# The first cross-attention of a two-layer decoder: head placement by DMA copies in place of zero-padded projections

## What is computed

```python
def _L0_xattn_ref(query, key_value, Wq, bq, Wk, bk, Wv, bv, Wo, bo):
    H = 16
    D = Cq // H                      # 256 // 16 = 16
    scale = D ** (-0.5)
    q = (query @ Wq + bq).reshape(B, Nq, H, D).transpose(0, 2, 1, 3)
    k = (key_value @ Wk + bk).reshape(B, Nkv, H, D).transpose(0, 2, 1, 3)
    v = (key_value @ Wv + bv).reshape(B, Nkv, H, D).transpose(0, 2, 1, 3)
    attn = jnp.clip(jnp.einsum('bhqd,bhkd->bhqk', q, k) * scale, -1e4, 1e4)
    attn = jax.nn.softmax(attn, axis=-1)
    x = jnp.einsum('bhqk,bhkd->bqhd', attn, v).reshape(B, Nq, Cq)
    return x @ Wo + bo

x = _layernorm(x + _L0_attn_ref(x, ...))
x = _layernorm(x + _L0_xattn_ref(x, ctx_768, ...))
```

## Time and profile before

| | us |
|---|---|
| median of three timed runs | 1267.47 (1267.25 to 1268.99) |
| the profiled execution | 1272.5 |
| its span | 1270.6 |
| PE busy | 1150.3 (91%) |
| DVE busy | 719.7 (57%) |
| ACT busy | 565.0 (44%) |
| POOL busy | 105.4 (8%) |

### The profile page before, as it was taken

One profiled execution on the slowest core, in us unless ns is written; L12 is line 12 of the kernel. 1 busy time (PEld: TensorE's weight loads), 2 busy tenths in 40 slices (PEclk: granted clock), 3 DMA queues, 4 the chain that ended last, 5 costly groups with the idle time before them and its releaser, 6 DMA issues.

```text
span 1270.6 us, 19991 instructions
## 1 busy us (share of the span) xinstructions
PE 1150.3 (91%) x7418; PEld 720.2 (57%) x7418; DVE 719.7 (57%) x1054; ACT 565.0 (44%) x1084; POOL 105.4 (8%) x147
## 2 busy tenths in 40 slices
PE   4999999898988988869988999999999999998797
PEld 2453443442222322247866777877787887786465
DVE  4344445667888789661426466465646666673213
ACT  1344344154545555751214566456635564562210
POOL 0112232112100000010001000010001000100100
PEclk7799899898979999979999999999999999999799
DMA  7012212320000000000023233123634964400000
GB/s 205 14 51 100 89 37 100 115 76 1 1 1 1 1 1 1 1 18 1 1 67 112 62 91 74 34 52 83 150 85 100 214 144 101 101 18 1 1 17 17
DMA packets 56962, 74.20 MB, mean 58 GB/s; under 512 B 12443, under 2 KB 33446, under 8 KB 56870
## 3 DMA queue, kind: packets, MB, share of 16 engines
q1 hardware_dynamic: 53110, 69.26, 21.4%
q10 hardware_dynamic: 3760, 3.67, 0.9%
HBM read 36.20 MB, written 15.73 MB: 41 GB/s over the span
## 4 chain that ended last, share of the span: by engine, by line
PE 79%; DVE 9%; issue 5%; ACT 4%; DMA 1%; POOL 1%; SPq 1%; ACTq 0%; POOLq 0%; DVEq 0%
PE p_unit L1665 20%; PE p_ring L1665 12%; PE p_out L1789 9%; PE p_ring L1685 8%; PE p_ring L1766 8%; PE p_ring L1732 7%; PE p_out L1755 6%; DVE halves L1454 2%; PE p_unit L1857 2%; PE p_ring L1710 1%; ACT prob_b L1238 1%; DVE prob_a L1468 1%; DVE x L1560 1%; PE p_ring L1724 1%; PE p_ring L1703 1%
## 5 line engine op out<-in xcount | busy, mean ns | idle before, releaser
L1454 DVE TENSOR_REDUCE halves<-p_ring 128x2 f32<-128x1024 f32 x128 | 156.2, 1220 | 65.8 <-PE p_ring L1710 65.6
L1252 ACT ACTIVATE prob_a<-p_ring 128x1024 f32<-128x1024 f32 x128 | 130.6, 1022 | 101.6 <-PE p_ring L1732 101.4
L1434 DVE TENSOR_REDUCE nmax<-p_ring 128x2 f32<-128x1024 f32 (+1 forms) x128 | 156.0, 1219 | 33.7 <-PE p_ring L1685 33.6
L1270 ACT ACTIVATE probT_b<-p_ring 128x512 f32<-128x512 f32 x144 | 84.5, 598 | 202.2 <-PE p_ring L1766 200.7
L1238 ACT ACTIVATE prob_b<-p_ring,nmax 128x512 f32<-128x512 f32 (+1 forms) x192 | 158.6, 837 | 18.3 <-DVE nmax L1434 18.0
L1685 PE MATMUL p_ring<-stacks 128*128 128x512 f32 x512 | 151.4, 418 | 8.9 <-ACT prob_b L1238 5.3
L1487 DVE COPY probT_b<-p_ring 128x512 f32<-128x512 f32 x112 | 77.1, 688 | 133.5 <-PE p_ring L1766 133.0
L1766 PE MATMUL p_ring<-ident,prob_b 128*128 128x128 f32 x1024 | 134.5, 274 | 0.3 <-ACT probT_b L1270 0.3
L1766 PEld LDWEIGHTS p_ring<-ident,prob_b 128*128 128x128 f32 x1024 | 116.2, 141 | 23.5 <-issue 14.8
L1732 PE MATMUL p_ring<-x_q,x_kq 32*128 32x512 f32 x512 | 124.4, 658 | 2.9 <-DVE halves L1454 2.9
L1454 DVE TENSOR_REDUCE wide_max<-p_ring 128x2 f32<-128x256 f32 (+3 forms) x64 | 52.6, 823 | 90.3 <-PE p_ring L1703 90.3
(11 more groups left out here) (226 smaller groups left out, 1614.1 us busy)
## 6 DMA issues: line engine op xcount, KB each, us to landing
stacks<-x_kd SPq DMA_DIRECT2D x64, 256.0 KB, 5.9
stacks<-splitH_b SPq DMA_DIRECT2D x80, 128.0 KB, 2.3
stacks<-splitL_b SPq DMA_DIRECT2D x80, 128.0 KB, 2.4
x_kd<-early SPq DMA_DIRECT2D x19, 256.0 KB, 2.0
x_v<-x_vd SPq DMA_DIRECT2D x8, 512.0 KB, 4.1
x_kd<-xT SPq DMA_DIRECT2D x13, 256.0 KB, 2.0
x_vd<-early SPq DMA_DIRECT2D x11, 256.0 KB, 2.0
a_st<-a_image SPq DMA_DIRECT2D x64, 32.0 KB, 1.8
```

Source lines behind the costliest of these rows:

```text
L1252: nc.scalar.activation(prob_place(key), slot_of("S2", key), ACT.Exp, accum_out=x0_sums[:, m:m + 1]).then_inc(done["E2"], 1)
L1270: keep_turned(act, key, lambda o, i: nc.scalar.activation(o, i, ACT.Copy)).then_inc(done["VA"], 1)
L1434: nc.vector.tensor_reduce(nmax[:, n % 4, 0:heads], src, AX.X, ALU.max, negate=True).then_inc(done["M"], 1)
L1454: nc.vector.tensor_reduce(to, src, AX.X, ALU.max, negate=True).then_inc(done["M1"], 1)
```

## The change

Queries and keys of X0 are now projected without padding. A batch takes four key units (`kd`: 128 of 256 rows of all heads, by 512 context rows) and two query units (`qd`), 12 in all in place of 24. `kd` goes to the early buffers and, by XO, to a tensor `x0_kd` in DRAM; `qd` goes to `x0_qd` in SBUF. A new step KL on SP, one for each group, then copies each head's 16 rows to its block of 32 in `x0_kq`: four DMAs from `x0_kd` and four from `x0_qd`. It waits for both stores, the queries, and the last S2 of group n − 3. One cast of 128×1536 (KF) follows two ticks later in the schedule. S1 and S2 read 17 rows of a block in place of 32. POOL fills `x0_kq` once at the start with ones and zeros (row 16 stays), DVE's memsets and spreading copies of the weights go, and the two landing tensors for weights go as well. The scale of the queries is applied by ACT as it drains them. The slots of the early buffers are dealt anew; both halves of an X1 key unit are stored after `EL`.

The diff, cut:

```diff
@@ paired_stream
-            if u[0] in ("k", "q") and u[1] == "X0":
-                sched.add("KF", *u)
-            if u[:2] == ("v", "X1"):
+            if u[:2] == ("v", "X1") or u[0] == "kd":
                 sched.add("XO", *u)
@@ build_schedule
+    def x0_keys(b):
+        return [unit("kd", b, m, s) for m in range(2) for s in range(2)]
+
+    def x0_queries(b):
+        return [unit("qd", b, m, after=[turned_x("A0", b)] + ([later(("KL", (0, 2 * m + 1)), 3)] if b else [])) for m in range(2)]
+
+    def x0_operands(b, g):
         n = 4 * b + g - HELD
+        return [step("KL", b, g, after=[UA("qd", b, g // 2), later(("XO", ("kd", b, g // 2, 1)), 1)]
+                     + (used(8 + n) if n >= 0 else [])),
+                step("KF", b, g, after=[later(("KL", (b, g)), 2)])]
...
+        order = [u[1][1:] for u in x0_keys(1)] + order
...
-                slot = sum(early_uses) % EARLY
+                slot = sum(early_uses) % (3 if u[:2] == ("kd", 0) else EARLY)
@@ SP
+                    if u[0] == "kd":
+                        _, b, m, s = u
+                        wait(sp, "UA", *u)
+                        sp.dma_start(x0_kd[b, 128 * m:128 * m + 128, 512 * s:512 * s + 512], early_place(u, 0))\
+                          .then_inc(early_out[early_places[(u, 0)][0]], 16)
...
-                        for part, ready in ((1, "EH"), (0, "EL")):
-                            wait(sp, ready, *u)
+                        wait(sp, "EL", *u)
+                        for part in (1, 0):
...
+                if kind == "KL":
+                    b, g = key
+                    G, place = 8 + 4 * b + g, (4 * b + g) % HELD
+                    sp.wait_ge(x0_cleared, 1)
+                    for s in range(2):
+                        slot, before = early_places[(("kd", b, g // 2, s), 0)]
+                        sp.wait_ge(early_out[slot], 16 * (before + 1))
+                    wait(sp, "UA", "qd", b, g // 2)
+                    if 4 * b + g >= HELD:
+                        wait(sp, "S2", *prob_items(PAIRS[G - HELD])[-1])
+                    for a in range(4):
+                        sp.dma_start(x0_kq[32 * a:32 * a + 16, place, 0:2, :],
+                                     x0_kd[b, 64 * g + 16 * a:64 * g + 16 * a + 16, :].rearrange("r (s n) -> r s n", s=2))\
+                          .then_inc(x0_held[place], 16)
+                        at = 64 * (g % 2) + 16 * a
+                        sp.dma_start(x0_kq[32 * a:32 * a + 16, place, 2, :], x0_qd[at:at + 16, g // 2, :])\
+                          .then_inc(x0_held[place], 16)
@@ POOL
-            pool.wait_ge(x0_scaled, 1)
+            nc.gpsimd.memset(x0_kq[:, :, 0:2, :], 1.0)
+            nc.gpsimd.memset(x0_kq[:, :, 2, :], 0.0).then_inc(x0_cleared, 1)
...
-                    wait(pool, "UA", *u)
-                    if 4 * b + g >= HELD:
-                        wait(pool, "S1", *max_items(PAIRS[8 + 4 * b + g - HELD])[-1])
-                    nc.gpsimd.tensor_copy(x0_kqF[:, place, part, :], x0_kq[:, place, part, :]).then_inc(done["KF"], 1)
+                    pool.wait_ge(x0_held[n % HELD], 16 * 8 * (n // HELD + 1))
+                    if n >= HELD:
+                        wait(pool, "S1", *max_items(PAIRS[8 + n - HELD])[-1])
+                    nc.gpsimd.tensor_copy(x0_kqF[:, n % HELD], x0_kq[:, n % HELD]).then_inc(done["KF"], 1)
@@ ACT
+                    elif u[0] == "qd":
+                        _, b, m = u
+                        act.wait_ge(x0_scaled, 1)
+                        if b:
+                            for g in (2 * m, 2 * m + 1):
+                                act.wait_ge(x0_held[g % HELD], 16 * 8 * (g // HELD + 1))
+                        ins = nc.scalar.activation(x0_qd[:, m, :], p_unit[:, :], ACT.Identity, bias=x0_bq[:, m:m + 1],
+                                                   scale=LAYERS["X0"]["D"] ** -0.5)
@@ DVE
-            nc.vector.memset(x0_wq[:, :, :], 0.0)
-            nc.vector.memset(x0_wk0[:, :], 0.0)
-            link(nc.vector.memset(x0_wk1[:, :], 0.0))
-            nc.vector.memset(x0_wk1[64:65, :].rearrange("p (h r) -> p h r", r=32)[:, :, 16], 1.0)
@@ PE, S1 (S2 alike)
-                            ins = nc.tensor.matmul(o[:, aa, :], x0_kqF[r:r + 32, place, 2, 128 * i:128 * i + 128],
-                                                   x0_kqF[r:r + 32, place, hf, :], start=True, stop=True,
+                            ins = nc.tensor.matmul(o[:, aa, :], x0_kqF[r:r + 17, place, 2, 128 * i:128 * i + 128],
+                                                   x0_kqF[r:r + 17, place, hf, :], start=True, stop=True,
```

More of the change, by code:

```diff
@@ L170, in may_score @@
             return age("DS", L, b, g) >= 3
-        return age("KF", "q", L, b, g) >= 2 and all(age("KF", "k", L, b, g, h) >= 2 for h in range(2))
+        return age("KF", b, g) >= 2
     def ready(item):
@@ L461, in build_schedule @@
         after_attention("A0", 1, "X0"),
[L462 to L465, removed]
+        [unit("cT", sg, c) for sg in range(2) for c in range(2)] + x0_keys(0)
+        + [unit("cT", sg, c) for sg in range(2, 4) for c in range(2)],
+        [q for b in range(B) for q in x0_queries(b)],
+        [s for b in range(B) for g in range(4) for s in x0_operands(b, g)],
         a0_start(1),
@@ L781, in decoder @@
         x1_kv_loaded = sem("x1_kv_loaded")
+        x0_cleared = sem("x0_cleared")
+        x0_held = [sem(f"x0_held{j}") for j in range(HELD)]
         wqk_ready = sem("wqk_ready")
@@ L1135, in _ @@
                 if kind == "KF":
[L1136 to L1142 removed]
+                    b, g = key
+                    n = 4 * b + g
+                    pool.wait_ge(x0_held[n % HELD], 16 * 8 * (n // HELD + 1))
+                    if n >= HELD:
+                        wait(pool, "S1", *max_items(PAIRS[8 + n - HELD])[-1])
+                    nc.gpsimd.tensor_copy(x0_kqF[:, n % HELD], x0_kq[:, n % HELD]).then_inc(done["KF"], 1)
                 elif kind == "EH":
@@ L1317, in _ @@
                         ins = nc.scalar.activation(a0_H[:, u[2], :], p_unit[:, :], ACT.Copy)
-                    elif u[0] in ("q", "k") and u[1] == "X0":
-                        _, L, b, g = u[:4]
-                        place, part = (4 * b + g) % HELD, u[4] if u[0] == "k" else 2
-                        if 4 * b + g >= HELD:
-                            wait(act, "S2", *prob_items(PAIRS[8 + 4 * b + g - HELD])[-1])
-                        if u[0] == "q":
-                            ins = nc.scalar.activation(x0_kq[:, place, part, :], p_unit[:, :], ACT.Identity,
-                                                       bias=x0_bq[:, g:g + 1])
-                        else:
-                            ins = nc.scalar.activation(x0_kq[:, place, part, :], p_unit[:, :], ACT.Copy)
-                    elif u[:2] in (("k", "X1"), ("v", "X1")):
+                    elif u[0] == "qd":
[6 more added lines that the diff above has]
+                                                   scale=LAYERS["X0"]["D"] ** -0.5)
+                    elif u[:2] in (("k", "X1"), ("v", "X1")) or u[0] == "kd":
                         early_free(act, u, 0)
@@ L1704, in _ @@
                     else:
-                        wait(pe, "KF", "q", L, b, g)
-                        wait(pe, "KF", "k", L, b, g, hf)
+                        wait(pe, "KF", b, g)
                         place = (G - 8) % HELD
@@ L1732, in _ @@
                             ins = nc.tensor.matmul(o[:, aa, :],
-                                                   x0_kq[r:r + 32, place, j // 4, 128 * (j % 4):128 * (j % 4) + 128],
-                                                   x0_q2[r:r + 32, G % 2, :], start=True, stop=True,
+                                                   x0_kq[r:r + 17, place, j // 4, 128 * (j % 4):128 * (j % 4) + 128],
+                                                   x0_q2[r:r + 17, G % 2, :], start=True, stop=True,
                                                    tile_position=(r, 0))
```

83 lines of the change are left out of this document (32 added, 51 removed).

## The result

| | median us | range, runs |
|---|---|---|
| before, beside it | 1268.95 | 1267.25 to 1271.73, 6 |
| changed | 1347.41 | 1338.41 to 1349.01, 6 |

The account below looks back on a forecast made before the run. In X0 PE sets the pace with a projection in each tick, DVE without. Terms −23.0 + 3.7 − 2.1 + 3.0 + 3.5 + 1.0 = −13.9 us took 1267.47 to 1253.6 us; range 1244 to 1264.

Parts of the forecast that it names:

- Part 4: X0's scores read 17 rows instead of 32, columns staying 512: nothing, ±1 us in all.
- D: Slower rival: every X0 cast holds a clip all its 1.6 us and brings a half-clock spell; 1272.6 us, chance 0.08.
- Part 1: Five triplets of projections leave X0's loop, 4.42 us each, 5.3 for the first: −23.0 us.
- Part 2: Projections that come back: one query unit at tick 107, two more units in ticks 90–103; +3.7 us.
- Part 3: At the start, memsets leave DVE ahead of a step PE waits for: −2.1 us, bounds 0 and −2.2.
- Part 5: KL's copies, eight DMA issues per group on SP, nothing urgent behind them in X0's loop: costed at nothing.
- Part 6: One fused POOL cast per group in X0: held DVE clips +3.0 us, one new half-clock spell +3.5 us.
- Part 7: Early buffer slots, ticks 93 and 94: ACT's writes of batch 1's x wait for stores; +1.0 us, bounds 0 and 3.
- Rival B: X0's new casts cost nothing, if they fall beside the row reduce: 1247 us, chance 0.20.
- C: Rival: three of five X0 casts bring a half-clock spell, two more than forecast; 1260.6 us, chance 0.17.
- E: Rival: SP queue jams before X0, ticks 64 to 70, so POOL and PE wait for copies; 1260.6 us, chance 0.10.
- wrong altogether: Sign in X0's loop: DMA copies come late, with PE waiting for KF at a group's first S1; no size given.

Follow-up runs that it names:

- 32-row kernel: The changed kernel with X0's scores S1 and S2 reading 32 rows again instead of 17, nothing else: 1246.4 us, ratio 0.982; second series 1241.2 us, 0.977.

## Why the prediction was wrong, point by point

- **Part 4, rows 17 instead of 32, is the step that failed.** It said "Nothing, ±1 us in all", from a duration at full clock: 524 ns for 17 rows in A0 against 506. As a duration that was right. In the changed kernel too S1 takes 0.50 us where the clock is whole, 0.79 where it isn't. What it left out, with no reason given, is that the granted clock can depend on what the matmuls read. The row it rested on was from A0, whose ticks hold projections beside the 17-row matmuls; I carried it to a loop that has none. The cost was 100 us (1347.4 against 1246.4), more than four times the sum of all gains, and no rival had it: D came out by its sign, 1272.6, but its mechanism (casts that hold clips, each with a spell) is not what happened, since three short casts change nothing. None of the forecast, the range and the chance of 0.08 for slower allowed for a term whose size no row of the kernel before bounded. The place to see the risk was in the prediction: it priced low-clock spells in two parts and never asked which edit changes what PE does.
- **Part 1, the triplets, −23.0: right.** The intervals of the 32-row kernel that answer to 35.36 and 38.56 us are 30.94 and 34.20: −4.42 and −4.36. Put back as dummies, the 15 units cost 22 to 29 us, in a single run.
- **Part 2, +3.7: not contradicted.** The interval with the added query unit, 36.01 before, is 33.06: −2.95, where −4.4 + 1.5 = −2.9 was worked out. The two units at ticks 90 to 103 share an interval with the first triplet, the slots and a spell (81.80 to 77.37 us, −4.4), and can't be told apart.
- **Part 3, the start, −2.1: too large.** The load took over the wait, the bound of zero that I had named. In the 32-row kernel, PE at the value projections:

```profile
20.49 3.30 PE L1675 MATMUL p_unit<-a_wv,xT 128*128 128x256 f32 x8 [3.05 <-DMA x_wo<-in_L_xattn_Wo]
```

3.05 us idle, ended by the landing of `x0_wo`, and the start at 20.49 instead of 19.90. In the trace of the changed kernel these matmuls start at 19.29, and `x0_wo` ends the wait there too; no trace without the memsets has them before 19.09. Of the memsets' 2.18 us 0.8 at the most were gained.
- **Part 5, the DMA copies, nothing: right.** In the 32-row kernel, in no interval of X0 did a group's first S1 wait for KF; empty intervals take 30.94 us as before.
- **Part 6, the casts, +3.0 and +3.5: both mis-sized, 0.** The mechanism was right: clips beside four of the five casts took 1.39, 1.27, 1.28 and 1.14 us in place of 0.69. But they cost nothing. Here POOL, DVE and PE around the fourth cast of the 32-row kernel:

```profile
404.46 1.47 POOL L1165 CAST x_kqF<-x_kq 128x1536 fp32r<-128x1536 f32 x1 [29.32 <-DMA x_kq<-x_qd]
...
405.33 1.14 DVE L1478 TENSOR_SCALAR prob_a<-prob_a 128x1024 f32<-128x1024 f32 x1
...
407.25 0.50 PE L1719 MATMUL p_ring<-x_kqF 32*128 32x512 f32 x2 [0.65 <-ACT prob_a L1275]
```

PE's wait behind it is 0.65 us, no longer than the 0.75 of a plain pair of ticks, and the interval that holds it is 30.94 us, the same to 0.01 as one without. The prediction's "DVE has no slack" was too strong: DVE is busy 19.30 of 20 us from 380 on, which by my estimate leaves about 1.1 us in an interval of 30.94, more than the 0.45 to 0.70 us that a clip was held. That this and the three buffers of the ring take up the delay is argued, not tested. Nor did a spell start right behind a cast. Of the long jobs the multiply did both: its interval fell by 6.7 us when it was cut, near the 4.45 + 3.5 = 8.0 that part 6 worked out for it.
- **Part 7, slots, +1.0: as said.** ACT's writes of `xT` for batch 1 in the 32-row kernel:

```profile
256.01 0.60 ACT L1338 ACTIVATE xT<-p_unit 128x512 f32<-128x512 f32 x1 [1.13 <-DMA x_kd<-xT]
...
259.60 0.60 ACT L1338 ACTIVATE xT<-p_unit 128x512 f32<-128x512 f32 x1 [1.98 <-DMA x_kd<-xT]
```

They waited 1.13 and 1.98 us for the stores; PE then waited 1.20 us for ACT. What of it reaches the span was not measured by itself.

With part 6 at zero and part 3 at its bound of zero, the sum is −23.0 + 3.7 + 1.0 = −18.3, and the 32-row kernel lay 21.6 and 25.5 under before. Rival B (1247) had this kernel's time, that of the 32-row kernel, though not by its reason: clips were held, only without effect. The mechanisms of rivals C, D and E were not seen; POOL waited up to 1.66 us for a copy of KL in A0, and PE never for POOL there. The condition under "wrong altogether" was not met either: the prediction named no sign in the profile by which its real failure could have been foreseen, though half clock in new windows was on its list, as a sign of spells behind casts.

## What to carry to other kernels

When an edit changes what a matmul reads, its partitions included, look at the granted clock of the stretch that it runs in and not only at its duration: fewer rows saved no time here and cost the clock of everything around them, and 15 more rows of ones against zeros were free and worth 100 us. A duration from a stretch with wide matmuls in it need not hold in a stretch without. And a delay seen on one engine (clips held for 0.45 to 0.70 us here) need not reach the span: compare whole intervals with and without it before you price it.

## What the hardware did that was not expected

- The granted clock follows the number of rows that matmuls contract, at the same columns and the same cycles. With both scores at 32 rows the loop without projections ran at 1.00 (2.4 GHz); at 17 rows it ran at 0.50 (1.2 GHz) for most of 350 us, and two ticks took 5.88 in place of 3.77 us. The table above gives the steps between. The Trainium skill ("TensorE: Matmul & The Clock Gate", Part 1: The HAM clock gate) ties the clock to how busy PE has been; busy time alone doesn't tell the two cases here apart: at 17 rows PE was busy 17.66 and 18.44 of 20 us from 360 and 560 on, at half clock, and at 32 rows 16.78 of 20 us from 380 on, at the whole clock.
- The fall needs no unusual gap. With the long POOL jobs in pieces it came at about 309 us behind waits of 0.98, 0.73 and 0.23 us, which left the clock at 1.00 with 32 rows. Behind a gap of 2.45 us both fell; with 32 rows the loop had the clock back some 8 us later.
- A POOL cast of 128×1536 takes 1.46 us, not three times 0.61 = 1.83, and four of them held a clip of DVE for 0.45 to 0.70 us each without a cost that shows in the loop; POOL's multiply of 5.7 us held one for 4 us (4.73 in place of 0.69), and the long jobs in pieces gained 6 to 12 us.
